# Reading a transposed value out of PSUM in a long-convolution stage, with four product buffers

## The reference

```python
kv = vr[:, :, :, None, :] * x2r[:, :, None, :, :]
k_f = jnp.fft.rfft(k.astype(jnp.float32), n=fft_size)
y = jnp.fft.irfft(jnp.fft.rfft(kv, n=fft_size) * k_f[None, :, None, None, :], n=fft_size)[..., :L]
skip = bias.astype(jnp.float32).reshape(H, num_heads)[None, :, :, None, None]
y = y + kv * skip
out = jnp.einsum('bhijl,bhil->bhjl', y, x1r)
...
x = x + jnp.tanh(g_xattn[0]) * _L0_xattn_ref(_layernorm(x, axis=-1), L0_xattn_k, fside_S2_0, ctx_2048, ctx_2048, 8)
```

## Time and profile before

| What | us |
|---|---|
| median of 3 runs (890.1, 895.25, 895.4) | 895.25 |
| profiled execution, its own time | 886.02 |
| its span | 884.3 |
| VectorE busy in the span | 618.5 |
| TensorE busy in the span (matmuls) | 787.3 |
| ScalarE busy | 319.5 |
| GpSimd busy | 171.2 |

### The profile page before, as it was taken

One profiled execution on the slowest core, in us unless ns is written; L12 is line 12 of the kernel. 1 busy time (PEld: TensorE's weight loads), 2 busy tenths in 40 slices (PEclk: granted clock), 3 DMA queues, 4 the chain that ended last, 5 costly groups with the idle time before them and its releaser, 6 DMA issues.

```text
span 884.3 us, 13802 instructions
## 1 busy us (share of the span) xinstructions
PE 787.3 (89%) x4627; PEld 629.2 (71%) x4627; DVE 618.5 (70%) x1196; ACT 319.5 (36%) x515; POOL 171.2 (19%) x185
## 2 busy tenths in 40 slices
PE   2887879699999999999997999976699999999994
PEld 2565657478888888888885455535588878888884
DVE  5999999754575466457546888897446785877764
ACT  2120212033333342342233777756143323334221
POOL 1999989700000000003000121211010000000000
PEclk9999999999999999999999999998589999999998
DMA  7221212000000000000101112110000000000000
GB/s 274 72 71 61 75 47 65 13 1 1 1 1 0 0 0 0 0 0 20 31 1 44 51 54 85 53 42 13 0 1 1 1 24 0 0 24 0 24 1 25
DMA packets 22133, 26.06 MB, mean 29 GB/s; under 512 B 5328, under 2 KB 17744, under 8 KB 21968
## 3 DMA queue, kind: packets, MB, share of 16 engines
q1 hardware_dynamic: 22096, 25.60, 9.2%
HBM read 23.22 MB, written 2.10 MB: 29 GB/s over the span
## 4 chain that ended last, share of the span: by engine, by line
PE 67%; DVE 20%; issue 8%; ACT 3%; POOL 1%; DVEq 1%; DMA 1%; SPq 0%; ACTq 0%; POOLq 0%
PE bank L1592 21%; PE bank L1460 19%; PE bank L1473 11%; PE bank L1523 2%; DVE A L864 2%; DVE A L875 2%; PE bank L1513 2%; DVE small L1071 1%; PE bank L1376 1%; PE bank L1601 1%; PE bank L1533 1%; DVE A L1081 1%; PE bank L1510 1%; PE bank L1377 1%; PE bank L1378 1%
## 5 line engine op out<-in xcount | busy, mean ns | idle before, releaser
L1592 PE MATMUL bank<-R 128*128 128x512 f32 (+3 forms) x1080 | 214.9, 360 | 11.4 <-DVE R L1235 4.9
L1592 PEld LDWEIGHTS bank<-R 128*128 128x128 f32 (+1 forms) x1080 | 180.8, 190 | 45.0 <-DVE R L1235 5.1
L1460 PE MATMUL bank<-R 128*128 128x512 f32 x768 | 186.2, 392 | 1.9 <-issue 1.9
L1460 PEld LDWEIGHTS bank<-R 128*128 128x128 f32 x768 | 140.4, 188 | 29.3 <-issue 2.2
L1019 DVE TENSOR_TENSOR A<-bank,A 128x512 f32<-128x512 f32 (+1 forms) x68 | 47.1, 692 | 113.1 <-PE bank L1460 110.8
L1473 PEld LDWEIGHTS bank<-R 128*128 128x128 f32 (+1 forms) x816 | 105.8, 190 | 10.5 <-issue 4.0
L1473 PE MATMUL bank<-R 128*128 128x256 f32 (+1 forms) x816 | 109.4, 284 | 2.5 <-DVE R L1029 2.2
L579 ACT ACTIVATE A<-bank 128x512 f32<-128x512 f32 (+1 forms) x68 | 40.6, 597 | 189.2 <-PE bank L1460 181.5
L1376 PE MATMUL bank<-A 128*128 128x256 f32 x128 | 45.1, 436 | 25.8 <-DVE A L864 17.6
L451 POOL TENSOR_TENSOR A<-A 128x256 f32<-128x256 f32 x64 | 64.1, 1001 | 10.3 <-DVE A L875 10.3
L1376 PEld LDWEIGHTS bank<-A 128*128 128x128 f32 x128 | 21.8, 202 | 44.7 <-DVE A L864 24.9
(11 more groups left out here) (172 smaller groups left out, 1129.4 us busy)
## 6 DMA issues: line engine op xcount, KB each, us to landing
A<-in_w SPq DMA_DIRECT2D x16, 384.0 KB, 3.0
A<-in_w SPq DMA_DIRECT2D x8, 480.0 KB, 3.6
A<-in_ctx_one SPq DMA_DIRECT2D x8, 272.0 KB, 3.6
A<-in_ctx_half SPq DMA_DIRECT2D x8, 256.0 KB, 3.1
A<-in_ctx_nat SPq DMA_DIRECT2D x4, 512.0 KB, 3.7
A<-in_ctx_t SPq DMA_DIRECT2D x128, 16.0 KB, 2.0
out<-X SPq DMA_DIRECT2D x4, 512.0 KB, 2.9
A<-in_filt SPq DMA_DIRECT2D x1, 1536.0 KB, 11.8
```

The lines of the kernel that those rows point to most:

```text
L1460: mm = nc.tensor.matmul(dst[0:pr], wX[:, j, at + k * P:at + k * P + pr], mX[:, k], start=(n == 0), stop=(n == 5))
L1592: mm = nc.tensor.matmul(dst, a, m, start=start and n == 0, stop=stop and n == len(prods) - 1, skip_group_check=skip)
```

## The change

The transposed value is no longer copied to SBUF: kv reads it out of PSUM, in bank 2 for groups 0 and 2 and in bank 1 for groups 1 and 3. ScalarE's `a_turned` and its semaphore are gone. The block sums move from bank 2 to bank 3, which the transposed sums use as well, so each of the two waits until the other has been read. kv has four buffers in the place of two and of `vT`, and is issued three heads ahead instead of two. Three convolutions of the next group instead of two stand ahead of `a_sum`. The skip products move from head 16 to head SKIP_A = 11. The loops of both engines in this stage are written out.

```diff
-TURN_A, BIAS_A = 6, 8
+TURN_A, BIAS_A, SKIP_A = 6, 8, 11
+AHEAD, KVS = 3, 4
...
-        (toep, ctxN, ctxT, vN, vT, kv_, zr_, z4, stg_) = carve(
-            A1, [NH0 * 2 * P, BG * D, BG * D, BG * D, BG * D, 1024, 1024, 8 * HALF * P, 2 * W0T])
+        (toep, ctxN, ctxT, vN, kv_, zr_, z4, stg_) = carve(
+            A1, [NH0 * 2 * P, BG * D, BG * D, BG * D, KVS * 512, 1024, 8 * HALF * P, 2 * W0T])
...
-        TV, WB, OB = bank[1], bank[2], bank[3]
+        TV, OB = [bank[2], bank[1]], bank[3]
+        WB = OB
...
-            def a_turned(g, first=False):
-                act.wait_ge(vtp_ready, g + 1)
-                if not first:
-                    act.wait_ge(kv_ready, NH0 * g)
-                for k in range(DT):
-                    nc.scalar.activation(vT[:, k * BG:(k + 1) * BG, :], TV[:, k * NT:(k + 1) * NT], ACT.Copy
-                                         ).then_inc(vT_ready, 1)
...
             def a_kv(g, h, first=False):
-                u = h % 2
+                u = h % KVS
                 t0 = h * I0
                 c = ctxT[:, h // 8, :, t0 % 64:t0 % 64 + I0]
+                v = TV[g % 2][:].rearrange("p (q t) -> p q t", t=P)
 
                 if not first:
-                    dve.wait_ge(y_ready, 1 + NH0 * g + h - 1)
+                    dve.wait_ge(y_ready, 1 + NH0 * g + h - AHEAD)
                 nc.vector.tensor_tensor(
-                    kv[:, u], vT[:, :, t0:t0 + I0].unsqueeze(3).to_broadcast([P, 8, I0, I0]),
+                    kv[:, u], v[:, :, t0:t0 + I0].unsqueeze(3).to_broadcast([P, 8, I0, I0]),
                     c.unsqueeze(2).to_broadcast([P, 8, I0, I0]), ALU.mult).then_inc(kv_ready, 1)
...
-                    if h + 2 < NH0:
-                        if h + 2 == NH0 // 2:
+                    if h + AHEAD < NH0:
+                        if h + AHEAD == NH0 // 2:
                             dve.wait_ge(ctxT_loaded[1], 16 * (g + 1))
-                        a_kv(g, h + 2)
+                        a_kv(g, h + AHEAD)
                     elif more:
-                        if h + 2 == NH0:
-                            dve.wait_ge(vT_ready, 2 * (g + 2))
+                        if h + AHEAD == NH0:
+                            dve.wait_ge(vtp_ready, g + 2)
                             dve.wait_ge(ctxT_loaded[0], 16 * (g + 2))
-                        a_kv(g + 1, h + 2 - NH0)
+                        a_kv(g + 1, h + AHEAD - NH0)
...
-                    if more and h == NH0:
+                    if more and h == SKIP_A:
                         a_skip(g + 1)
...
-            with dve.Fori(0, G - 2) as g:
-                step.enter(g, per, start)
+            for g in range(G - 2):
                 a_heads(g, True)
                 a_finish(g)
...
             def a_turn(g, first=False):
                 pe.wait_ge(vN_ready, BG * (g + 1))
-                if not first:
-                    pe.wait_ge(vT_ready, 2 * g)
+                if g > 1:
+                    pe.wait_ge(kv_ready, NH0 * (g - 1))
...
                 if not first:
                     pe.wait_ge(t_done, g)
+                    pe.wait_ge(a_done, 1 + 2 * (g - 1))
...
             def a_sum(g):
 
                 pe.wait_ge(z2_ready, 1 + NH0 * (g + 1))
-                pe.wait_ge(a_done, 1 + 2 * g)
+                pe.wait_ge(t_done, min(g + 2, G))
...
-            with pe.Fori(0, G - 1) as g:
-                for h in range(2, NH0):
+            for g in range(G - 1):
+                for h in range(2 if g == 0 else LEAD, NH0):
                     a_conv(g, h)
...
-                for h in range(2):
+                for h in range(LEAD):
                     a_conv(g + 1, h)
                 a_sum(g)
```

More of the change, by code:

```diff
@@ L149, in flamingo_kernel @@
         ctxT = ctxT.rearrange("p (s q t) -> p s q t", s=2, q=8)
-        vT = vT.rearrange("p (q t) -> p q t", t=P)
-        kv = kv_.rearrange("p (u q i j) -> p u q i j", u=2, q=8, i=I0)
+        kv = kv_.rearrange("p (u q i j) -> p u q i j", u=KVS, q=8, i=I0)
         zr = zr_.rearrange("p (u q i j) -> p u q i j", u=2, q=8, i=I0)
@@ L266, in flamingo_kernel @@
         ln_ready, vN_ready = sem("ln_ready"), sem("vN_ready")
-        vtp_ready, vT_ready, bvx_ready, w_ready, t_done = (
-            sem("vtp_ready"), sem("vT_ready"), sem("bvx_ready"), sem("w_ready"), sem("t_done"))
+        vtp_ready, bvx_ready, w_ready, t_done = sem("vtp_ready"), sem("bvx_ready"), sem("w_ready"), sem("t_done")
         zh_ready = sem("zh_ready")
@@ L528, in _ @@
             a_prep(0, True)
-            a_turned(0, True)
             with act.Fori(0, G - 1) as g:
@@ L535, in _ @@
                     split_high(g, c)
-                a_turned(g + 1)
             def c_norm_one(g, b):
@@ L904, in a_heads @@
                 route = Steps() if more else group_route(0)
+                if more and g < G - 2:
+                    norm_of = lambda: group_norm(g + 2, gate[:, 0:1])
+                elif more:
+                    norm_of = lambda: group_norm(0, None)
                 for h in range(LEAD, NH0 + LEAD if more else NH0):
@@ L912, in a_heads @@
                         dve.wait_ge(vN_ready, BG * (g + 2))
-                        if not isinstance(g, int):
-                            norm = group_norm(g + 2, gate[:, 0:1])
-                        elif more:
-                            norm = group_norm(0, None)
+                        norm = norm_of()
                     beside = norm if norm.left() else route if h > 8 else Steps()
                     beside.take(1 if more else 2)
-                    if h + 2 < NH0:
-                        if h + 2 == NH0 // 2:
+                    if h + AHEAD < NH0:
+                        if h + AHEAD == NH0 // 2:
                             dve.wait_ge(ctxT_loaded[1], 16 * (g + 1))
-                        a_kv(g, h + 2)
+                        a_kv(g, h + AHEAD)
                     elif more:
-                        if h + 2 == NH0:
-                            dve.wait_ge(vT_ready, 2 * (g + 2))
+                        if h + AHEAD == NH0:
+                            dve.wait_ge(vtp_ready, g + 2)
                             dve.wait_ge(ctxT_loaded[0], 16 * (g + 2))
-                        a_kv(g + 1, h + 2 - NH0)
+                        a_kv(g + 1, h + AHEAD - NH0)
                     beside.take(1 if more else 2)
@@ L1279, in _ @@
             norm.take_all()
-            dve.wait_ge(vT_ready, 2)
+            dve.wait_ge(vtp_ready, 1)
             dve.wait_ge(ctxT_loaded[0], 16)
-            for h in range(2):
+            for h in range(AHEAD):
                 a_kv(0, h, True)
@@ L1286, in _ @@
                 a_z(0, h, h < 2)
-                a_kv(0, h + 2)
+                a_kv(0, h + AHEAD, h + AHEAD < KVS)
                 if h == 1:
@@ L1291, in _ @@
             dve.wait_ge(small_loaded, 16 * 3)
-            per = N_STATS + 1
-            start = step.value()
-            with dve.Fori(0, G - 2) as g:
-                step.enter(g, per, start)
+            for g in range(G - 2):
                 a_heads(g, True)
                 a_finish(g)
-            step.leave(per, G - 2, start)
             a_heads(G - 2, True)
@@ L1373, in a_conv @@
                 diag, off = toep[:, h, 0:P], toep[:, h, P:2 * P]
-                kv0 = kv[:, u, 0:BG].rearrange("p q i j -> p (q i j)")
-                kv1 = kv[:, u, BG:2 * BG].rearrange("p q i j -> p (q i j)")
+                kv0 = kv[:, h % KVS, 0:BG].rearrange("p q i j -> p (q i j)")
+                kv1 = kv[:, h % KVS, BG:2 * BG].rearrange("p q i j -> p (q i j)")
                 nc.tensor.matmul(y[:, 0:n], diag, kv0, start=True, stop=False, skip_group_check=True)
@@ L1743, in d_tiles @@
                     d_delta(g + 1, 0)
-            for h in range(2, NH0):
+            for h in range(LEAD, NH0):
                 a_conv(G - 1, h)
```

2 lines of the change are left out of this document (1 added, 1 removed).

## The result

| | us | ratio to before |
|---|---|---|
| before, median of 4 runs (890.1 to 895.4) | 892.69 | 1 |
| changed kernel, median of 4 runs (876.15 to 880.02) | 877.88 | 0.9844 (0.9807 to 0.9882) |
| before, profiled execution | 886.02 | |
| changed kernel, profiled execution | 876.32 | |

The account below looks back on a forecast made before the run. VectorE was taken to limit the convolution stage, much of its busy time being waits against GpSimd. Terms 5.8 + 5.6 + 0.9 + 1.4 + 4.6 - 8.0 - 3.3 = 7.0 us less, 895.25 to 888; range 877 to 896.

Parts of the forecast that it names:

- kv, +5.8: 64 kv products on VectorE: reading PSUM takes each from 815 to 679 ns, 8.7 us less a third struck.
- the doubled read: Rival at kv: the repeated PSUM read costs double, 27 us lost, 922 us; chance 0.03.
- The small steps, +5.6: VectorE's small operations behind kv: 0.37 us each gained, five of seven pairs a group, three groups.
- The bias, +0.9: Bias product at head 8 (1.83 us): gains 0.3 us in each of three groups.
- The turn, +4.6: Last z to next group's z(3): 9.26 us in place of 10.79, 1.53 gained in each of three groups.
- The skip, -8.0: Skip products moved to head 11, where VectorE is the limit: 2.66 us lost in each of three groups.
- The clock, -3.3: TensorE's clock falls after standing about 4.3 us behind L838 and the skip: 1.1 us lost in each of three groups.
- The slower rival: TensorE stays at 1.2 GHz from head 11 through the turn: 21 us lost against 7 gained, 909; chance 0.05.
- First and last group: Last group's term: 0.37 us on four small operations, +1.4; heads 3 to 8 there, no gain.
- The port is freed altogether: Rival: all seven pairs gain, no half clock, last group gains twice as much; 14 us, about 881; chance 0.32.
- A new limit: Rival: GpSimd falls behind, normalised values come late, VectorE waits 0.8 us a group; 896; chance 0.15 with kv not freed.

Follow-up runs that it names:

- kv_psum: Kernel before with only kv reading its value (the first group's, in every group) from PSUM, ScalarE's copies gone; 873.06 us, ratio 0.9802.
- ahead2: Changed kernel with the depth undone: kv two heads ahead, two convolutions of the next group ahead of the transposed sums; 879.98 us, ratio 0.9865.
- conv0: Changed kernel, but the next group's first convolution waits for z 14 instead of z 15; 875.29 us, ratio 0.9811.
- kv_sbuf: Changed kernel with kv reading an SBUF tensor of the same shape instead of the value in PSUM; 895.66 us, ratio 1.0026.
- own_bank: Changed kernel with block sums in the finished value's banks, not shared with the transposed sums, and skip back at head 16; 868.22 us, ratio 0.9750.

## Why the prediction was right in sign and half in size

**kv, +5.8.** Right as a mechanism: flat at 678, nothing over 693. The repeated PSUM read costs nothing extra, and the doubled read is refuted. The Trainium skill's price for a PSUM source (VectorE: DVE Perf Modes, the TRN2 errata), 62 cycles or an estimated 65 ns each, does not appear in an operation with one input in each memory: the medians are 679 before and 678 after. There was reason to strike a part of the 8.7, though no run measures how much. In kv_psum kv and the two small steps of a turn are 1.25 us shorter, and the turn only 0.51 (10.28 against 10.79); heads 3 to 8 of its last group take 10.29 where they took 10.70.

**The small steps, +5.6.** This is the term that failed. Summed over the stage (columns: busy us, mean ns), before and after, the two most common of those behind a kv or a split:

```profile
L836 DVE TENSOR_TENSOR tmp<-tmp,ve 128x4 f32<-128x4 f32 x9 | 6.1, 679 | 0.0
...
L838 DVE TENSOR_SCALAR tmp<-tmp 128x4 f32<-128x4 f32 x9 | 6.3, 695 | 0.0
```

```profile
L826 DVE TENSOR_TENSOR tmp<-tmp,ve 128x4 f32<-128x4 f32 x9 | 2.1, 230 | 0.0
...
L828 DVE TENSOR_SCALAR tmp<-tmp 128x4 f32<-128x4 f32 x9 | 4.5, 497 | 0.0
```

L836 lost 4.0 us, L838 1.8. With L843 (4.8 to 1.4), L845 (3.8 to 2.4), L828 (2.1 to 0.7) and L840 (1.4 to 0.5), which become L833, L835, L818 and L830, the six have gone from 24.5 to 11.6: 12.9 where I had 5.6. Each pair's small step gave 0.45 and not 0.37, and all seven gave it, though between heads 10 and 11 z then waits 0.53 for its convolution. I had counted GpSimd late until head 11, because its split behind head 5 sets it back by 1.80; the trace has its add waiting for z at 74.28, in step already at head 9. The row of 80.93 in the earlier trace rows, waiting 0.36 for z of the same head, had said so before. It catches up during the bias product, which holds VectorE for 1.8. The step behind the split (1.78 to 1.18) and the last one (1.25 to 0.80) gave another 1.05 a group, which I had not priced.

8.7 and 12.9 are 21.6, and kv_psum gained 18.8. The difference has gone into waits: over the stage VectorE stood idle before z for 6.9 us, and in kv_psum for 10.5. No run divides the 18.8 between the product and the small steps.

The prediction also misread what the small steps are. It says that they "still have two SBUF inputs", but L828 and L838 are TENSOR_SCALAR with one (`rs<-rs`, `tmp<-tmp`), and they stood like the others: 0.69 and 1.78, where L838 two heads later takes 0.16.

```profile
89.88 0.16 DVE L838 TENSOR_SCALAR tmp<-tmp 128x4 f32<-128x4 f32 x1
```

What makes such a step stand was not tested; two SBUF inputs are not needed for it.

**The bias, +0.9.** Nothing: 1.82 after, 1.83 before. It still meets GpSimd's add, whoever was late before it.

**The turn, +4.6.** Right: 9.17 us against 9.26 said, in the order said. What I did not see is that the skip had been nearly free there.

**The skip, -8.0.** 2.39 against 2.66, so -7.2; it waits for nothing.

**The clock, -3.3.** In the first two groups nothing: TensorE stands 3.05 us before 82.58, not the 4.3 that I had said, and the granted clock of 84 to 88 is 1.00. In the third it fell, behind a stop of 3.06:

```profile
84.00:88.00 4.00, 2.68 (x12) 2.08 (x12) 3.53 (x10) 0.00 (x0) 3.43 (x6) 1.00 0.00 0
...
116.00:120.00 4.00, 3.85 (x9) 3.16 (x10) 3.17 (x11) 0.38 (x1) 2.51 (x5) 0.50 0.00 0
```

That group took 35.69, 2.1 more than the second. So a stop of 3 us lowered the clock once in three times, and a stop of 1.93 did so before. I had set today's low stretches as given and only counted new ones; kv_psum, without any, suggests that they were part of the price of the two SBUF inputs: TensorE's stop for kv behind the split is 1.17 us there and was 1.93. It is one execution, and ahead2 and conv0, with kv in PSUM as well, do have low stretches. The slower rival stayed away; the low level never reached the sums of these groups.

**First and last group.** From 28.91 to 67.24 the first group took 38.33, and now (28.94 to 62.28) 33.34, 5.0 less. From its z(3) to the stage's end the last one took 35.5 and now takes 32.7, 2.8 less where I had 1.4; nearly all of it is in heads 9 to 15 (16.12 to 13.66). The sum is closed: 5.0 + 4.1 + 2.0 + 2.8 = 13.9 against 13.8.

**The rivals.** "The port is freed altogether" gave 14, and that is the size that came, for its reasons in the main: the seven pairs, no low clock in two groups of three, and 2.8 from the last group, twice 1.4. That it is 14 to the microsecond is partly luck, since the third group's low clock took 2.1 back, the bias gave nothing, and the steps that it had not priced gave more. Nor is the port freed altogether: the bias product and the step behind the split still stand. The sentence of the Trainium skill behind it (SBUF — State Buffer, "Who interferes with whom": one SBUF input outside the two-port modes does not contend) holds in all 64 kv. "A new limit" did not come, though it was near: ScalarE delivers the normalised values 9.2 us behind the last z (95.90), and VectorE asks for them behind z(4) at 97.9. That the rest of the change would cost 5 us was in the terms (4.6 - 8.0 - 3.3 = -6.7), and kv_sbuf shows 5.5.

## What to carry to other kernels

When an engine is "busy", compare the minimum, median and maximum of one instruction: a long tail on an operation with two SBUF inputs beside GpSimd work is a wait. Here moving one input to PSUM removed it, for the operation and for GpSimd, and most of it for the small steps behind both, whose busy time fell by more than the operation's own (12.9 us against 8.7). When buffers then have to be shared, look for the stretch where another engine paces and leave the displaced work there: the same skip cost its full 2.4 us among the heads, and own_bank's turn with it inside is 0.45 longer than the changed kernel's without it. And measure each part alone; the change as a whole hid that its edits other than the operand cost 5 us together, though the depth by itself gained.

## What the runs showed of the hardware that I had not expected

- A VectorE product that reads each PSUM element eight times in a row (broadcast in the innermost step) takes 678 ns for 512 columns, as much as one from SBUF or one that repeats its SBUF operand.
- GpSimd's 128 x 256 add has a median of 0.73 us when free, and 1.13 when it alternates with a two-SBUF-input VectorE product: the two then take turns.
- A VectorE step of 4 columns with a single SBUF input (L838) took 1.78 us beside GpSimd's 1.80 us split, and 0.16 at 89.88 in the same group.
- TensorE's granted clock did not follow the length of the last stop: 1.00 behind stops of 3.06 and 3.05 us, 0.50 behind one of 3.06 at the same place in the third group, 0.61 behind 1.93 in the kernel before. What decides between these was not settled.
- The same program behind the stage took 408.5 to 413.7 us in twelve profiled executions, and the shortest was the one from which the prediction was made.
